# Attention scores as three products of 64 rows, two heads on the two row halves of the array

## The reference

```python
q = (x @ Wq.T).reshape(b, t, N_HEAD, HS).transpose(0, 2, 1, 3)
q = q.reshape(b, N_KV, GROUP, t, HS)
k = (x @ Wk.T).reshape(b, t, N_KV, HS).transpose(0, 2, 1, 3)
...
att = jnp.einsum('bkgqd,bkjd->bkgqj', q, k) * scale
att = jnp.where(mask[None, None, None, :, :], att, -jnp.inf)
att = jax.nn.softmax(att, axis=-1)
y = jnp.einsum('bkgqj,bkjd->bkgqd', att, v)
```

## Time and profile before

| | |
|---|---|
| median of three runs | 2591.63 us |
| the profiled execution | 2589.44 us, its span 2587.6 us, granted clock 0.956 |
| busy, share of the span: TensorE, VectorE, ScalarE, GpSimd | 91%, 57%, 39%, 5% |
| masks (L903) | 512, 335.6 us |
| exponentials (L547) | 512, 353.8 us |
| copies out of `t_ps` (L539) | 480, 286.8 us |
| transposes of probabilities (L718) | 2112, 343.3 us |
| scores products with `k_hi` and with `k_lo` (L703) | 768 each, 273.3 and 227.9 us |

### The profile page before, as it was taken

The page is one execution under the profiler, slowest core; times in us unless marked ns, Lnnn a source line. Parts: engine busy times, 40 slices in busy tenths (PEclk is TensorE's granted clock), DMA queues, the critical chain, the costliest instruction groups (busy, mean ns, idle before and its releaser), DMA issues. The chain is left out here.

```text
span 2587.6 us, 34615 instructions
## 1 busy us (share of the span) xinstructions
PE 2356.0 (91%) x13464; PEld 1751.0 (68%) x13464; DVE 1476.2 (57%) x2976; ACT 1015.5 (39%) x1998; POOL 132.7 (5%) x289
## 2 busy tenths in 40 slices
PE   3799999799999978999978999996799999999998
PEld 3666666576666666666657666662688888888887
DVE  3545555456555544555545555552576666767666
ACT  2245555435555523556552456552321211211111
POOL 1100000010000010000001000000011110101000
PEclk6899999899999989999989999997799999999999
DMA  8542444314423432353341332432512221222221
GB/s 318 203 151 93 146 143 156 129 64 157 151 104 126 161 118 100 111 177 127 127 173 68 139 124 97 159 129 95 187 68 81 81 81 61 68 81 73 81 71 43
DMA packets 88374, 311.82 MB, mean 121 GB/s; under 512 B 16153, under 2 KB 32537, under 8 KB 72369
## 3 DMA queue, kind: packets, MB, share of 16 engines
q1 hardware_dynamic: 81904, 286.95, 31.3%
q0 software_dynamic: 4608, 16.78, 2.0%
q10 hardware_dynamic: 1728, 6.29, 0.7%
HBM read 263.82 MB, written 46.17 MB: 120 GB/s over the span
## 5 line engine op out<-in xcount | busy, mean ns | idle before, releaser
L539 ACT ACTIVATE pt<-t_ps 128x512 f32<-128x512 f32 x480 | 286.8, 597 | 528.6 <-PE t_ps L718 528.2
L903 DVE CUSTOM_DVE_ANT_0 probs<-s_ps,mask 128x644 f32<-128x644 f32 (+5 forms) x512 | 335.6, 659 | 232.9 <-PE s_ps L703 230.4
L718 PE MATMUL t_ps<-ident,probs 128*128 128x128 f32 (+1 forms) x2112 | 343.3, 286 | 67.5 <-ACT pt L539 51.3
L547 ACT ACTIVATE probs<-probs,neg_max 128x644 f32<-128x644 f32 (+5 forms) x512 | 353.8, 691 | 49.2 <-DVE neg_max L903 43.6
L718 PEld LDWEIGHTS t_ps<-ident,probs 128*128 128x128 f32 (+1 forms) x2112 | 231.6, 138 | 198.3 <-ACT pt L539 109.4
L653 PE MATMUL j_ps<-x_hi,w 128*128 128x512 f32 x960 | 329.3, 410 | 0.0
L703 PE MATMUL s_ps<-k_hi,q 128*128 128x512 f32 (+4 forms) x768 | 273.3, 356 | 16.8 <-DVE neg_max L903 16.8
L1206 PE MATMUL out_ps<-wo,by_hi 128*128 128x512 f32 x1024 | 277.2, 392 | 0.0
L739 PE MATMUL o_ps<-pt,v 128*64 128x256 f32 x1920 | 242.9, 395 | 0.0
L920 DVE TENSOR_SCALAR probs<-probs,inv_sum 128x644 f32<-128x644 f32 (+5 forms) x512 | 229.0, 469 | 8.7
L739 PEld LDWEIGHTS o_ps<-pt,v 128*64 128x64 f32 x1920 | 129.7, 140 | 153.7 <-issue 104.9
(11 more groups left out here) (148 smaller groups left out, 3059.4 us busy)
## 6 DMA issues: line engine op xcount, KB each, us to landing
fw<-in_L_ffn_d_w_dram SPq DMA_DIRECT2D x128, 1024.0 KB, 4.9
w<-WT SPq DMA_DIRECT2D x40, 1024.0 KB, 7.2
probs<-in_L_attn_x_dram POOLq DMA_DIRECT2D x32, 512.0 KB, 4.1
Y<-y SPq DMA_DIRECT2D x128, 128.0 KB, 3.0
b_x<-in_L_attn_x_dram SPq DMA_DIRECT2D x32, 512.0 KB, 4.3
b_y<-Y SPq DMA_DIRECT2D x32, 512.0 KB, 5.8
out_dram<-b_res SPq DMA_DIRECT2D x32, 512.0 KB, 5.1
WT<-w_split SPq DMA_DIRECT2D x12, 1024.0 KB, 10.3
```

The lines of the kernel that those rows point to most:

```text
L539: act.activation(dst, src.rearrange("p (h q) -> p h q", q=P), ACT.Copy).then_inc(pt_ready, 1)
L547: act.activation(probs[:, slot, 0:width], probs[:, slot, 0:width], ACT.Exp, bias=neg_max[:, slot:slot + 1], scale=-1.0, accum_out=row_sum[ ...
L718: last = pe.transpose(t_ps[0:rows_, bass.ts(head, P)], probs[:, GROUP * (u % 2) + head, P * i:P * i + rows_], ident[:, :])
L903: dve.tensor_tensor_reduce(out=probs[:, slot, 0:width], in0=s_ps[head % 2][:, 0:width], in1=m, scale=-SCALE, scalar=-NEG, op0=ALU.add, op1 ...
```

## The change

The queries are split 128 rows at a time: `q_hi` and `q_lo` are the two halves of the old tile `q` (the first and the last two of its four parts), and each holds a pair of heads, one in either half of the partitions. `q_copies` and `q_low` become one instruction of 128 partitions each. The function `scores` now does a pair of heads: for each piece, three products (hi with `k_hi`, hi with `k_lo`, lo with `k_hi`) of 64 rows for each head, one head on the upper and one on the lower row half, alternating, into `s_ps[0]` and `s_ps[1]`. The fourth product, lo with `k_lo`, is dropped. The pair takes both tiles at once, so it waits for both masks before it, and counts both heads at its end. The order changes with it: TensorE does pair 0 in round 0 and pair 1 in round 3; ScalarE does the exponentials behind copies 1, 2, 4 and 5; VectorE does both divisions of pair 0 before masks 2 and 3.

```diff
         q = sb("q", [P, GROUP, T], F32R)
+        q_hi, q_lo = q[:, 0:GROUP // 2, :], q[:, GROUP // 2:GROUP, :]
...
                     act.wait_ge(q_full, 4 * KV * b + piece + 1)
-                    for head in range(2):
-                        h = slice(HS * head, HS * head + HS)
-                        last = act.activation(q[h, 2 * pair + head, bass.ts(ch, BANK)], piece_bank(piece)[h, :], ACT.Copy)
-                    last.then_inc(q_hi_ready, 1)
+                    act.activation(q_hi[:, pair, bass.ts(ch, BANK)], piece_bank(piece)[:, :], ACT.Copy
+                                   ).then_inc(q_hi_ready, 1)
...
                             take_turned(b, s - 1, i)
-                        if 1 <= i < 5 and s < UNITS:
-                            exponentials(b, s, i - 1)
+                        if i in (1, 2, 4, 5) and s < UNITS:
+                            exponentials(b, s, i - 1 - (i > 3))
...
-                def scores(b, s, head):
+                def scores(b, s, pair):
...
-                    if s % 4 == 0 and head % 2 == 0:
-                        pe.wait_ge(q_lo_ready, 4 * KV * b + 2 * (s // 4) + head // 2 + 1)
+                    if s % 4 == 0:
+                        pe.wait_ge(q_lo_ready, 4 * KV * b + 2 * (s // 4) + pair + 1)
...
-                    if s or head >= 2:
-                        pe.wait_ge(masked, GROUP * u + head - 1)
-                    out = s_ps[head % 2]
-                    lhs = q[:, head, bass.ts(qb, P)]
+                    if s or pair:
+                        pe.wait_ge(masked, GROUP * u + 2 * pair)
                     first = qb - n + 1
...
                         width = (blocks.stop - blocks.start) * keys
-                        for part, k in enumerate((k_hi, k_lo)):
-                            last = pe.matmul(out[:, o:o + width], lhs, k[:, g, blocks, 0:keys],
-                                             start=part == 0, stop=part == 1)
-                    last.then_inc(scores_ready, 1)
+                        for m, (qs, k) in enumerate(((q_hi, k_hi), (q_hi, k_lo), (q_lo, k_hi))):
+                            for head in range(2):
+                                h = slice(HS * head, HS * head + HS)
+                                last = pe.matmul(s_ps[head][:, o:o + width], qs[h, pair, bass.ts(qb, P)],
+                                                 k[h, g, blocks, 0:keys], start=m == 0, stop=m == 2)
+                    last.then_inc(scores_ready, 2)
...
                             turn_probs(b, s - 1, i)
-                        if i < GROUP:
-                            scores(b, s, i)
+                        if i in (0, 3):
+                            scores(b, s, i // 3)
...
                     dve.wait_ge(q_hi_ready, 4 * KV * b + piece + 1)
-                    for head in range(2):
-                        hi = slice(HS * head, HS * head + HS)
-                        lo = slice(HS * (1 - head), HS * (1 - head) + HS)
-                        last = dve.tensor_tensor(q[lo, 2 * pair + head, bass.ts(ch, BANK)], piece_bank(piece)[hi, :],
-                                                 q[hi, 2 * pair + head, bass.ts(ch, BANK)].bitcast(F32), ALU.subtract)
-                    last.then_inc(q_lo_ready, 1)
+                    dve.tensor_tensor(q_lo[:, pair, bass.ts(ch, BANK)], piece_bank(piece)[:, :],
+                                      q_hi[:, pair, bass.ts(ch, BANK)].bitcast(F32), ALU.subtract
+                                      ).then_inc(q_lo_ready, 1)
...
                     mask_scores(b, s, 0)
                     mask_scores(b, s, 1)
-                    mask_scores(b, s, 2)
                     invert(b, s, 0)
                     divide(b, s, 0)
+                    divide(b, s, 1)
+                    mask_scores(b, s, 2)
                     mask_scores(b, s, 3)
-                    divide(b, s, 1)
                     invert(b, s, 1)
```

## The result

The changed kernel takes 2654.6 us (median of four runs, 2646.9 to 2663.3) where the kernel before takes 2590.7 us beside it: 1.0246 times as long, 95% interval 1.0208 to 1.0283. It is slower by about 64 us; the forecast was 2608 us, slower by 18. The profiled execution has a span of 2651.0 us, 63.4 more than before. The way and the range held, the size didn't: the pair of heads cost more than the sum had for it.

What follows compares the result with a forecast made beforehand. Attention was taken as bound by TensorE's order of work, with rounds of at least 1.34 us. Conversions -12.8, step order and products +20.6, last steps +10.4 gave +18 us: 2608 us predicted, range 2565 to 2672.

Steps and rivals of the forecast that it cites:

- Conversion of queries: At each batch start, merged copies and subtractions let scores start earlier: gain 3.2 us, 12.8 us in 4 batches.
- Side by side: In the scores, two 64-row halves load and compute together like column strips: three slots per piece instead of four.
- weight loads one after another: Rival, chance 0.13: in the scores, products overlap but each 128-column load takes its own 0.11 us; 2672 us.
- halves in turn: Rival, chance 0.07: in the scores, row halves run in turn, 1.38 us per 512-column piece; about 2805 us.
- The price of the layout change: Around each pair's scores on TensorE: 0.10 us for entry and some 0.09 us for leaving, from 0.14 at column strips.
- X: TensorE time of a wide pair's scores with entry and exit: 1.16 us against 1.44 before, bounds 0.97 and 1.25.
- my 23 us for each 0.1 us of X: Whole-kernel sensitivity to a pair's scores time: about 230 pairs reach a step's end, 23 us per 0.1 us.
- 20.6 + 10.4 = 31: Attention steps: +20.6 us from 16 groups of steps, +10.4 us from the last steps of 4 batches.
- The order: Attention steps with pairs in rounds 0 and 3, later masks waiting for exponential 1: +1.3 us per group, +20.6 us.
- Block 3's chain: Query block 3's step: masks, exponentials, inverse and divisions set its end at 9.75 us, before 8.53, +1.2 us.
- Block 5: Query block 5's step: TensorE would end at 10.4 us, the mask-to-division chain at 10.7; change 0.
- The last four steps: Each batch's end, without projections: blocks 4 and 5 end at 10.1 us, 6 and 7 grow 0.35 each; +10.4 us overall.

Runs made afterwards that it cites:

- The two pairs of runs that differ in conversions and products: New order with old products and conversions against the changed kernel: 2667.1 against 2654.6 us; both with projections only in rounds without scores: 2590.1 against 2580.5 us.
- the kernel with half rows: Kernel before, same order and number of scores products, each reading only rows 0 to 63 of queries and keys: 2704.7 us, 1.0437.
- The kernel with the order alone: Kernel before with the changed kernel's order, but the old four 128-row products and old 64-row conversions: 2667.1 us, 1.0300.

## Why the prediction was right, and where it was off

**Conversion of queries: right.** Forecast 3.2 us per batch start, measured 8.74 - 5.58 = 3.16 us in batch 0. The other three are alike (8.70 to 8.73 before, 5.57 to 5.62 after), so 12.5 us in all. The two pairs of runs that differ in conversions and products (12.5 and 9.6 us) agree within the swing of the stages between batches. But the number hid a second part. TensorE's idle time fell by 2.74 - 0.93 = 1.81 us. Behind the 2.74 us of standing, the granted clock from 158.6 to 161.7 us was 0.52, near the lower of its two levels (1.2 GHz), and the projection products stood 0.43 to 0.53 us apart. After the change it is 1.00 from 155 to 162 us. My sum took 0.23 us for each product and so counted this gain without naming it.

**Side by side: right.** Column strips were a good guide to how row strips work, though not to their price. The rivals with weight loads one after another and with halves in turn are out: the short slots stand 0.11 us apart for two products, and taking the halves' independence away costs 240 us. That the time fell near the 2672 us of the rival on weight loads says nothing for it.

**The price of the layout change: the term that was mis-sized.** I took 0.14 us from the change between two column layouts, and let X = 1.16 us contain 0.10 for the way in and 0.09 for the way out, with 1.25 as its bound. Measured: the 0.10 us of the first product after transposes stay, 0.18 come on top before it, 0.09 on the way out, and 0.06 at the next projection product, which I hadn't counted at all. That makes 1.36 us, or 1.42 where a projection follows, against 1.44 for two heads before. The saved slot (0.23 + 0.11 us) and the layout change (0.29 to 0.35 us) cancel. At my 23 us for each 0.1 us of X the missing 0.20 to 0.26 us are 46 to 60 us.

The Trainium skill ("TensorEngine Tiling (Array Packing)", Key Properties) says that a change of tiling mode drains TensorE. The trace agrees that a change costs time: 0.29 to 0.35 us per way in and out in the kernel with half rows; that it is a drain, no row shows.

**The whole: closer than its parts.** The steps of the four batches sum up to 317.6, 318.9, 318.9 and 317.7 us before and to 340.9, 340.9, 338.7 and 338.2 after. That is 85.7 us more, where my sum had 20.6 + 10.4 = 31; the missing 55 us fit the term above. The rest of the kernel got 22.3 us shorter, not 12.8. Most of the difference lies in the stages between batches: 108.0, 107.8 and 111.5 us before at granted clocks of 0.89, 0.89 and 0.86, and 106.0, 102.0 and 101.9 after at 0.92, 0.95 and 0.95. The kernel with the order alone has the old conversions and is 9 us shorter there too. Why the clock differs no run shows; that this brought the total nearer to my 2608 us is luck.

**The order: right in kind.** Block 3's chain was put at 9.75 us and came to 10.01, released by the division after 1.32 us of idle time; block 1 at 6.2 and 6.52; block 2's gain at 0.8 and 0.6; the empty round of block 6 stands in the profile with its 0.69 us. The sum per group was 1.3 us and is 4.9 us; the rest is the step with X above, in blocks 4 to 7 (+0.84, +0.75, +0.88, +0.42 against +0.3, 0, +0.3, -0.3). Block 5 went wrong in kind as well: I had its end at the chain with TensorE done 0.3 us earlier, and both moved by 0.75 us, as pair 1 came later.

**The last four steps: too small as well.** I put blocks 4 and 5 at 10.1 us each; the first transposes of the steps s = 28 to 30,

```profile
458.62 0.66 PE L719 MATMUL t_ps<-ident,probs 128*128 128x128 f32 x4 [1.33 <-DVE probs L918]
...
468.89 0.66 PE L719 MATMUL t_ps<-ident,probs 128*128 128x128 f32 x4 [1.11 <-DVE probs L918]
...
479.33 0.66 PE L719 MATMUL t_ps<-ident,probs 128*128 128x128 f32 x4 [0.26 <-DVE probs L918]
```

give 10.27 and 10.44 us. Blocks 6 and 7 were to grow by 0.35 us each and grew by 0.85, from 11.13 to 11.98 us and alike: pair 1 overfills its round by more than I had reckoned, as X is longer. A group of eight steps grew by 4.8 to 4.9 us and these last seven steps by 6.1, so 16 x 4.86 us is too little for the steps. The rest of the 85.7 us, some 3 us, are steps at a lower granted clock, such as 0.58 from 332 to 339 us.

**What I called the cause.** I priced the change as products with an order around them. The runs turn this round: the order alone costs 74 us, and the new products win back only the conversions. What makes the order dear is that a round can't be under 1.34 us, so scores in it are nearly free up to some 0.9 us, and a pair of 1.36 us is not. Filling the emptied rounds gives 74 us back, part of which the kernel before could gain as well. Pairs in one go were forced by the row halves; that is the link between the change and its loss.

## What to carry to other kernels

Where an engine goes round a loop that another one paces (here transposes and the copy of 1.34 us), work inside the loop is free up to the slack, so two pieces merged into one cost more than two apart; put what fills next to where the holes are, before any product is made cheaper. A count of slots saved is no gain until the ways in and out are in the sum, also at the instruction after.

## What the hardware showed that I had not expected

The way into and out of a 64-row layout costs 0.18 us before the first product, 0.09 us after the last and 0.06 us at the next product of 512 columns (the first two in three kernels alike). Two heads on two row halves take 0.50 us where one takes 0.48, with 0.23 us to the next pair. At the batch start the granted clock was 0.52 for some 3 us behind 2.74 us of standing, and 1.00 where TensorE had stood 0.93 us. And spreading the projection two by two took 45 us off the kernel before, with the very same instructions.
